# One piece of W per step, contexts loaded ahead of the layouts, and two parts of W's rounding moved from VectorE to GpSimd

## The chip, the cores and the metric

The kernel runs on one core of a Trainium2 chip (trn2). The metric is the device time of one execution in microseconds (us). Three executions of the kernel before took 529.82, 531.11 and 535.19 us, median 531.11 us; a fourth, profiled one took 529.71 us.

## The reference

For each of 16 items b (256 rows, 256 columns):

```
x1  = x + attention(layernorm(x), ctx, ctx)         # 16 heads of 16 columns, softmax over 256 keys
out = x1 + ffn(layernorm(x1))
ffn(z) = q(silu(q(z) @ q(w_gate).T) * (q(z) @ q(w_up).T)) @ q(w_down).T
q(z):  per block of 16 columns   scale = max(max|z| / 6, 1e-12)
       z/scale rounded to the grid 0, .5, 1, 1.5, 2, 3, 4, 6 with its sign, times scale
```

The weights w_gate and w_up (704 x 256) and w_down (256 x 704) have to go through q once. The change is about this quantisation of the weights.

## The kernel before

**Stages.** Attention runs first (about the first 285 us of the trace), the feed-forward part over 32 tiles of 128 rows after it. Attention is a software pipeline of steps t = -3 to 16. In step t, TensorE (PE) computes, head by head, the scores of item t (L1098) and, 22 heads ahead, the raw scores of items t+1 and t+2 from which VectorE (DVE) takes row maxima (L1112 and L783, `max_scores` and `maximum`). ScalarE (ACT) takes exponents (L611), PE multiplies by the values (L1130, one call of 16 matmuls per four heads). Every engine walks the same grid of positions (g, j), g and j from 0 to 3, one head per position; a few other operations are hung on given positions. There are two PSUM banks MX: `max_scores` of a head waits until the maximum of the head two before it is taken.

**The order on each engine is the program's.** A wait holds up everything behind it on that engine. The only DMA queue is that of SyncE (SP).

**SP, step t:** wait for GpSimd's third part of the keys of item t+3 (`k_low`), issue 6 DMAs of 128 KB that stack them (L300, KS<-KP); wait for the transposed maxima, issue one small DMA (L368, QS<-MT), without which PE can't start step t+1; wait for the third part of the queries of item t+3 (`q_out`, which ACT makes at position (3, 3), its last), issue 6 DMAs (L300, QS<-QP); then the layouts of item t+5 (L285 QN and L287 KT), the context of item t+2 (L290 C), the rows of item t (L293 X), and what is due of the weights. As `q_out` comes at the end of step t, everything from the query stack on is issued while PE, DVE, ACT and GpSimd (POOL) are already in step t+1.

**Loads of W, before:** w_gate before and in step -1; w_up 384 KB at the end of SP's step 0 and 256 + 64 KB at the end of step 1; w_down 352 KB each at the end of steps 2 and 3.

**W's quantisation.** W has 4608 columns (gate, up, down, each 1536), cut into 16 slices of 288 columns. Slice t+1 is scaled in step t (offset SCALE = 1) and slice t is rounded in step t (offset GRID = 0):

- DVE at (1, 1): `weight_maxima` (L846, wmax); at (2, 2) `weight_limits` (L830 and L831); at (2, 3) `weight_inverses` (L835) and `round_weights` (L857, WC = max(WC, constant)); in steps -1 and 0 the three parts of the scaling stand at (3, 3).
- ACT at (0, 3): WC = |W| * constant (L652).
- POOL near the end of its step: W + WC (L486), - WC (L489), * scale (L492); then W * inverse of the next slice (L498).

POOL's step t in order: add the attention result to x (L443 twice), KR (L450), small statistics (L456 to L461), the third key part KP (L465, which gives `k_low`), the values VA from the context (L471), then the four of W.

**Step 15** has no further maxima. In it PE transposes W into 14 lots (L1144, one at each of the first 14 positions), ACT and DVE copy them out (L680, L862). Lots 11 to 13 need slice 15 finished (`w_done`). Two early steps of the feed-forward part's preparation stand before step 15 on every engine.

Of the kernel before, what the change touches and what calls it, by code (L numbers as in the profile page):

```python
# [92 lines left out]
def program(nc, x, x_p, ctx_in, ctx_t, wg_in, wu_in, wd_in, out):  # L93
# [8 lines left out]
    with es:  # L102
# [6 lines left out]
        def sem(name):  # L109
            return es.enter_context(nc.semaphore(name))  # L110
# [74 lines left out]
        def bank(p):  # L185
# [28 lines left out]
        o_den, o_norm, x1_ready = sem("o_den"), sem("o_norm"), sem("x1_ready")  # L214
        w_zeroed, w_begun, w_loaded = sem("w_zeroed"), sem("w_begun"), [sem(f"w_loaded{m}") for m in range(3)]
        w_seq, w_scaled, w_abs, w_c, w_grid, w_done = (sem(n) for n in
            ("w_seq", "w_scaled", "w_abs", "w_c", "w_grid", "w_done"))
        ones_ready, ones_last = sem("ones_ready"), sem("ones_last")
        w_tr, w_out = sem("w_tr"), sem("w_out")
# [63 lines left out]
        def _(sp):  # L283
# [22 lines left out]

            def load_last(m, w):
                full = FI // 128
                sp.dma_start(WN[m][0:FI - full * 128, full, :], w[full * 128:FI, :]).then_inc(w_loaded[m], 16)

            def load_down(r):
                sp.dma_start(WD[:, r, 0:FI], wd_in[128 * r:128 * (r + 1), :]).then_inc(w_loaded[2], 16)

            def load_weights(t):

                if t == -1:
                    load_blocks(0, wg_in, 2, 5, w_loaded[0])
                    load_last(0, wg_in)
                if t == 0:
                    load_blocks(1, wu_in, 0, 3, w_loaded[1])  # L320
                if t == 1:
                    load_blocks(1, wu_in, 3, 5, w_loaded[1])
                    load_last(1, wu_in)
                if t in (2, 3):
                    load_down(t - 2)

# [29 lines left out]
            def attention_step(st):  # L356
                if st.has(LEAD):
                    r = st.slot(LEAD, RING)
                    sp.wait_ge(k_low, st.times(LEAD, 1, 1))
                    gate(sp)  # L360
                    sp.wait_ge(sc_ready, st.times(0, H, 1))
                    gate(sp)
                    stack(KS[r], KP[st.slot(LEAD, 2)], (0, 1, 2, 0, 1, 0), r)
                if st.has(1):
                    sp.wait_ge(mt_ready, st.times(1, 1, 1))
                    gate(sp)
                    r = st.slot(1, 2)
                    sp.dma_start(QS[st.slot(1, RING)][PROD:ROWS, :, :].rearrange("d h t -> d (h t)"),  # L368
                                 MT[r][:, :]).then_inc(m_stacked[r], 16)
                if st.first == -1:  # L370
                    load_context(1, 1)
                    load_weights(-1)
                if st.has(LEAD):
                    sp.wait_ge(q_out, st.times(LEAD, 3, 3))
                    gate(sp)
                    stack(QS[r_q(st)], QP[st.slot(LEAD, 2)], (0, 0, 0, 1, 1, 2), r_q(st))
                if st.has(LOADS):
                    load_first(st.item(LOADS), st.slot(LOADS, RING))
                if st.first >= 0 and st.has(2):
                    load_context(st.item(2), st.slot(2, RING))  # L380
                if st.has(0):
                    load_x(st.item(0), st.slot(0, RING))
                if st.first >= 0:
                    load_weights(st.first)

# [10 lines left out]

            steps(sp, attention_step, -1, RING, 1, RING, B - 1, B)
            attention_step(Step(B - 1, B, RING))
            attention_step(Step(B, B, RING))
            ffn_steps(sp, ffn_step)  # L400
# [4 lines left out]
        def _(pool):  # L405
# [30 lines left out]
            def attention_step(st):  # L436
# [40 lines left out]
                if st.first == -1:  # L477
                    pool.wait_ge(v_ready, 1)
                    pool.wait_ge(m_parts, 1)
                    rows_of_ones((2,))  # L480
                if st.has(GRID):

                    ws = wslice(st, GRID)
                    pool.wait_ge(w_c, st.times(GRID, 1, 1))
                    gate(pool)
# [8 lines left out]
                if st.has(SCALE):  # L494
                    ws = wslice(st, SCALE)
                    pool.wait_ge(w_seq, st.times(SCALE, 4, 4))
                    gate(pool)
# [274 lines left out]
        def _(dve):  # L772
# [53 lines left out]

            def limits(amax, scale, inv, sem_, per, first, st, off):

                dve.wait_ge(sem_, st.times(off, per, first))
                nc.vector.tensor_scalar(scale, amax, 1 / 6, TINY, ALU.mult, ALU.max).then_inc(sem_, 1)  # L830
                nc.vector.tensor_scalar(inv, amax, UP / 6, TINY * UP, ALU.mult, ALU.max).then_inc(sem_, 1)  # L831

            def invert(inv, sem_, per, first, st, off):
                dve.wait_ge(sem_, st.times(off, per, first + 2))
                nc.vector.reciprocal(inv, inv).then_inc(sem_, 1)  # L835

            def weight_maxima(st):
# [3 lines left out]
                elif st.first == 0:  # L841
                    dve.wait_ge(w_loaded[0], 32)
# [6 lines left out]
            def weight_limits(st):  # L849
                limits(wmax[:, :], wscale[st.slot(SCALE, 2)][:, :], winv[:, :], w_seq, 4, 1, st, SCALE)  # L850
# [27 lines left out]
            def attention_step(st):  # L878
# [3 lines left out]
                for g in range(NG):  # L882
                    for j in range(HG):
                        maximum(st, g, j)
                        if (g, j) == (0, 3) and st.has(LEAD) and st.first > 2 - LEAD:
                            statistics(st)
                            aggregate(st)
                        if (g, j) == ((1, 1) if st.first > 0 else (3, 3)) and st.has(SCALE):
                            weight_maxima(st)
# [6 lines left out]
                        if (g, j) == ((2, 2) if st.first > 0 else (3, 3)) and st.has(SCALE):  # L896
                            weight_limits(st)
# [7 lines left out]
                        if (g, j) == (3, 3) and st.first == RING:  # L905
                            dve.wait_ge(w_loaded[2], 32)
                        if st.first == B - 1 and HG * g + j < LOTS:
# [426 lines left out]
```

## Time and profile before

| | |
|---|---|
| median of 3 executions | 531.11 us (529.82 to 535.19) |
| profiled execution, its own time | 529.71 us |
| its span, first to last instruction | 527.9 us |
| mean granted TensorE clock | 0.981 |
| busy: PE, DVE, ACT, POOL | 92%, 82%, 71%, 57% of the span |
| PE matmuls | 4036, 486.9 us |
| DVE row maxima L783 | 256, 164.2 us |
| DMA moved | 48.97 MB, all of it but instructions on one queue |

Each share is a mean over the whole span. Attention and the feed-forward part each have their own limit, and in attention the first steps, the middle ones and the last have theirs; so the numbers that matter are those of single steps. A row of a timeline gives start and duration in us, the engine, the line of the kernel, the operation and its tiles, how many instructions are merged (x6) and, in brackets, how long the engine sat idle before it and what ended that. SPq is SP's queue of DMA issues: its rows are the times that SP spends on issuing, not those of the transfers.

### The profile page before, as it was taken

Reading aid. Unit: us, or ns where it says so; the run is one execution under the profiler, and the core shown is the slowest. Engines: PE = TensorE matmul, PEld = TensorE weight load, DVE = VectorE, ACT = ScalarE, POOL = GpSimd, SP = SyncE. Lnnn points to the kernel's source line nnn. Section 1 sums busy time; section 2 is a strip of 40 time slices with the busy share of each in tenths; the row PEclk is TensorE's granted clock in tenths of the full one; section 3 lists DMA queues with packets and bytes.
Section 4 is the critical chain, followed back from the end, with each engine's and each line's share of the span. In section 5 each row is a group of like instructions: output and inputs, shape, how many; then the busy total and the mean of one; then the engine's idle time right before and its main releaser. Section 6 shows DMA issues by size and latency. Waiting matters only on the chain.

```text
span 527.9 us, 13628 instructions
## 1 busy us (share of the span) xinstructions
PE 486.9 (92%) x4036; PEld 383.1 (73%) x4036; DVE 435.1 (82%) x1129; ACT 373.8 (71%) x740; POOL 302.3 (57%) x423
## 2 busy tenths in 40 slices
PE   1889899999999999997857899999999999999996
PEld 0245565666666666654437899999999999999996
DVE  3788899899999999886345888898889998889764
ACT  5569899999999999977653565556656566665653
POOL 7754465556566665443144566666676666766542
PEclk9999999999999999999877899999999999999999
DMA  7784878766666666521000000000000000000000
GB/s 215 215 220 126 212 197 220 226 192 178 191 185 182 176 186 179 149 88 43 0 2 0 2 21 20 10 20 20 20 20 10 20 20 20 20 10 21 23 21 30
DMA packets 49985, 48.97 MB, mean 93 GB/s; under 512 B 4768, under 2 KB 47648, under 8 KB 49952
## 3 DMA queue, kind: packets, MB, share of 16 engines
q1 hardware_dynamic: 49952, 48.58, 32.8%
q8 instruction: 15, 0.25, 0.2%
q14 instruction: 18, 0.15, 0.1%
HBM read 18.94 MB, written 4.19 MB: 44 GB/s over the span
## 4 chain that ended last, share of the span: by engine, by line
PE 73%; DVE 7%; issue 5%; POOL 4%; SPq 4%; ACT 4%; DMA 3%; POOLq 0%; DVEq 0%; ACTq 0%
PE SC L1182 22%; PE PV L1182 12%; PE PV L1130 9%; PE MX L1112 9%; PE SC L1098 7%; DVE MF L783 4%; PE T L1207 4%; SPq L300 3%; DMA QS<-MT 2%; PE T L1212 2%; PE T L1077 2%; PE T L1045 2%; PE SC L1207 1%; PE T L1052 1%; ACT P L611 1%
## 5 line engine op out<-in xcount | busy, mean ns | idle before, releaser
L783 DVE TENSOR_REDUCE MF<-MX 128x2 f32<-128x512 f32 x256 | 164.2, 685 | 19.0 <-PE MX L1112 16.2
L611 ACT ACTIVATE P<-SC 128x512 f32<-128x512 f32 x256 | 140.3, 594 | 19.8 <-PE SC L1098 17.8
L1112 PE MATMUL MX<-KS,QS 96*128 96x256 bf16 x512 | 102.9, 284 | 4.3 <-DVE MF L783 2.5
L1098 PE MATMUL SC<-QS,KS 98*128 98x256 bf16 x512 | 98.5, 274 | 3.6 <-DMA QS<-MT 3.5
L534 POOL TENSOR_TENSOR HQ<-HN,hscale 128x704 f32<-128x704 f32 x31 | 43.1, 1391 | 61.3 <-DVE HN L936 61.3
L716 ACT ACTIVATE HH<-T 128x768 fp32r<-128x768 f32 x31 | 25.2, 813 | 67.9 <-PE T L1207 67.9
L1130 PE MATMUL PV<-P,VA 128*32 128x256 f32 x1024 | 70.0, 392 | 0.9 <-ACT OT L620 0.9
L1098 PEld LDWEIGHTS SC<-QS,KS 98*128 98x128 bf16 x512 | 43.4, 97 | 35.7 <-ACT P L611 20.0
L1182 PE MATMUL SC<-WH,XH 128*128 128x352 f32 x256 | 68.7, 350 | 0.0
L1112 PEld LDWEIGHTS MX<-KS,QS 96*128 96x128 bf16 x512 | 43.9, 99 | 31.6 <-DVE MF L783 23.3
L1182 PE MATMUL SC<-WH,XL 128*128 128x352 f32 x256 | 62.9, 327 | 0.0
L1182 PE MATMUL SC<-WL,XH 128*128 128x352 f32 x256 | 62.9, 327 | 0.0
L1130 PEld LDWEIGHTS PV<-P,VA 128*32 128x32 f32 x1024 | 27.3, 110 | 25.6 <-ACT P L611 7.1
L1182 PEld LDWEIGHTS SC<-WL,XH 128*128 128x128 f32 x256 | 45.6, 192 | 0.0
L1182 PEld LDWEIGHTS SC<-WH,XL 128*128 128x128 f32 x256 | 45.3, 191 | 0.1
L521 POOL TENSOR_TENSOR HN<-HN,hinv 128x704 f32<-128x704 f32 x31 | 43.1, 1390 | 1.0 <-DVE hinv L1026 0.9
L916 DVE TENSOR_TENSOR HN<-SC,SG 128x352 f32<-128x352 f32 x64 | 33.3, 521 | 11.3 <-PE SC L1182 10.1
L1182 PEld LDWEIGHTS SC<-WH,XH 128*128 128x128 f32 x256 | 41.4, 194 | 1.6
L685 ACT ACTIVATE SG<-SC 128x352 f32<-128x352 f32 x64 | 29.4, 460 | 18.0 <-PE SC L1182 13.4
L529 POOL TENSOR_TENSOR frstd<-fve,mhalf 128x2 f32<-128x2 f32 x32 | 22.1, 691 | 22.5 <-DVE fve L983 22.5
L486 POOL TENSOR_TENSOR W<-W,WC 128x288 f32<-128x288 f32 (+1 forms) x16 | 12.7, 796 | 38.8 <-DVE WC L857 38.8
L576 ACT ACTIVATE QP<-T 128x512 bf16<-128x512 f32 x48 | 28.6, 595 | 6.5 <-PE T L1052 3.6
(138 smaller groups left out, 1029.8 us busy)
## 6 DMA issues: line engine op xcount, KB each, us to landing
KS<-KP SPq DMA_DIRECT2D x96, 128.0 KB, 3.1
QS<-QP SPq DMA_DIRECT2D x96, 128.0 KB, 2.4
QN<-in_x_p SPq DMA_DIRECT2D x16, 256.0 KB, 3.1
KT<-in_ctx_t SPq DMA_DIRECT2D x16, 256.0 KB, 3.1
C<-in_ctx SPq DMA_DIRECT2D x16, 256.0 KB, 4.2
X<-in_x SPq DMA_DIRECT2D x16, 256.0 KB, 4.9
out<-OB SPq DMA_DIRECT2D x32, 128.0 KB, 1.7
W<-in_L_ffn_w_down SPq DMA_DIRECT2D x2, 352.0 KB, 6.0
```

The lines of the kernel that those rows point to most:

```text
L521: nc.gpsimd.tensor_tensor(blocks(HN[r][:, :]), blocks(HN[r][:, :]), each(hinv[r][:, :]), ALU.mult).then_inc(hm_ready, 1)
L534: nc.gpsimd.tensor_tensor(blocks(HQ[r][:, 0:FI]), blocks(HN[r][:, :]), each(hscale[r][:, :]), ALU.mult).then_inc(hq_ready, 1)
L576: nc.scalar.activation(parts[:, n, :], bank, ACT.Copy).then_inc(out_sem, 1)
L611: nc.scalar.activation(P[g % 2][:, j, :, :], SC[h % 3][:, :, :], ACT.Exp, scale=0.25).then_inc(exp_done, 1)
L685: nc.scalar.activation(SG[a][:, :], G, ACT.Silu).then_inc(silu_done, 1)
L783: nc.vector.tensor_reduce(MF[st.slot(off, 2)][:, :, h:h + 1], MX[h % 2][:, :, :], AX.X, ALU.max, negate=True).then_inc(mx_done, 1)
L916: nc.vector.tensor_tensor(HN[st.slot(0, 2)][:, a * FH:(a + 1) * FH], U, SG[a][:, :], ALU.mult).then_inc(h_done, 1)
L1098: last = nc.tensor.matmul(SC[h % 3][:, k, :], KS[r][0:ROWS, h, k * 128:(k + 1) * 128], QS[r][0:ROWS, h, :], start=True, stop=True)
L1112: last = nc.tensor.matmul(MX[h % 2][:, q, :], QS[r][0:PROD, h, q * 128:(q + 1) * 128], KS[r][0:PROD, h, :], start=True, stop=True)
L1130: last = nc.tensor.matmul(PV[32 * j:32 * (j + 1), g % 2, :], VA[r][:, k, HG * g + j, :], P[g % 2][:, j, k, :], start=(k == 0), stop=(k == ...
L1182: mm = nc.tensor.matmul(dst, x[:, c, :], w[:, c, :], start=(first and i == 0), stop=(last and i == len(chunks) - 1))
L1207: return nc.tensor.matmul(dst, src, ident[:, :], start=first, stop=False, is_transpose=True, skip_group_check=True)
```

## The change

Weights are loaded in pieces of one block (128 KB; w_down in halves of a row block), one at the end of each of SP's steps 1 to 8, 10 and 11. At the end of SP's step t-1, SP waits until the piece issued one step earlier has landed and raises `w_ready` to t. In step t (from 1 on) DVE waits at (1, 1) for `w_ready` >= t before it takes the maxima of slice t+1; before, it waited in steps 0, 4 and for w_down in step 4 only. The context of item t+3 instead of t+2 is loaded, and before the layouts. Step 0's scaling moves from (3, 3) to (1, 1). DVE's `weight_limits` (two operations on 128x18) and `round_weights` (one on 128x288) go to POOL: the limits after VA and before the rounding of W, the rounding's max in front of L486; `weight_inverses` waits for them and stands at (3, 0). SP's steps are written out one by one without a loop.

```diff
+            PIECES = {t + 1: t for t in range(FI // 128 + 1)}
+            DOWN = {7: (0, 0, 384), 8: (0, 384, FI), 10: (1, 0, 384), 11: (1, 384, FI)}
+            def load_piece(t):
+                done = w_piece[t % 3]
+                if t in DOWN:
+                    load_down(*DOWN[t], done)
+                elif t in PIECES and PIECES[t] < FI // 128:
+                    load_blocks(1, wu_in, PIECES[t], PIECES[t] + 1, done)
+                elif t in PIECES:
+                    load_last(1, wu_in, done)
+            def piece_landed(t):
+                turns = sum(1 for u in (*PIECES, *DOWN) if u <= t - 2 and u % 3 == (t - 2) % 3)
+                if turns:
+                    sp.wait_ge(w_piece[(t - 2) % 3], 16 * turns)
+                sp.sem_inc(w_ready, 1)
...
                     stack(QS[r_q(st)], QP[st.slot(LEAD, 2)], (0, 0, 0, 1, 1, 2), r_q(st))
+                if st.has(LEAD):
+                    load_context(st.item(LEAD), st.slot(LEAD, RING))
                 if st.has(LOADS):
                     load_first(st.item(LOADS), st.slot(LOADS, RING))
-                if st.first >= 0 and st.has(2):
-                    load_context(st.item(2), st.slot(2, RING))
                 if st.has(0):
                     load_x(st.item(0), st.slot(0, RING))
-                if st.first >= 0:
-                    load_weights(st.first)
+                load_piece(st.first)
+                if 1 <= st.first + 1 < B:
+                    piece_landed(st.first + 1)
...
-            steps(sp, attention_step, -1, RING, 1, RING, B - 1, B)
-            attention_step(Step(B - 1, B, RING))
-            attention_step(Step(B, B, RING))
+            for t in range(-1, B + 1):
+                attention_step(Step(t, B, RING))
...
+                if st.has(SCALE):
+                    pool.wait_ge(w_seq, st.times(SCALE, 2, 1))
+                    pool.wait_ge(w_scaled, st.times(SCALE, 1))
+                    gate(pool)
+                    nc.gpsimd.tensor_scalar(wscale[st.slot(SCALE, 2)][:, :], wmax[:, :], 1 / 6, TINY,
+                                            ALU.mult, ALU.max).then_inc(w_lim, 1)
+                    nc.gpsimd.tensor_scalar(winv[:, :], wmax[:, :], UP / 6, TINY * UP, ALU.mult, ALU.max).then_inc(w_lim, 1)
                 if st.has(GRID):
                     ws = wslice(st, GRID)
+                    pool.wait_ge(w_abs, st.times(GRID, 1, 1))
+                    gate(pool)
+                    nc.gpsimd.tensor_scalar(WC[:, :], WC[:, :], MAGIC * ONE, None, ALU.max).then_inc(w_c, 1)
...
-                elif st.first == RING:
-                    dve.wait_ge(w_loaded[1], 48)
+                else:
+                    dve.wait_ge(w_ready, st.times(0, 1))
...
             def weight_inverses(st):
-                invert(winv[:, :], w_seq, 4, 1, st, SCALE)
-            def round_weights(st):
-                dve.wait_ge(w_abs, st.times(GRID, 1, 1))
-                nc.vector.tensor_scalar(WC[:, :], WC[:, :], MAGIC * ONE, None, ALU.max).then_inc(w_c, 1)
+                dve.wait_ge(w_lim, st.times(SCALE, 2, 2))
+                nc.vector.reciprocal(winv[:, :], winv[:, :]).then_inc(w_seq, 1)
...
-                        if (g, j) == ((1, 1) if st.first > 0 else (3, 3)) and st.has(SCALE):
+                        if (g, j) == ((1, 1) if st.first >= 0 else (3, 3)) and st.has(SCALE):
                             weight_maxima(st)
...
-                        if (g, j) == ((2, 3) if st.first > 0 else (3, 3)) and st.has(SCALE):
+                        if (g, j) == ((3, 0) if st.first >= 0 else (3, 3)) and st.has(SCALE):
                             weight_inverses(st)
-                        if (g, j) == (2, 3) and st.has(GRID):
-                            round_weights(st)
```

## Rows read from the trace of the kernel before

**Rows 1.** Timeline of PE: first score matmuls of steps 1 to 5, 8, 11, 12
```profile
47.34 0.39 PE L1098 MATMUL SC<-QS,KS 98*128 98x256 bf16 x2 [0.66 <-DMA QS<-MT]
...
63.14 0.39 PE L1098 MATMUL SC<-QS,KS 98*128 98x256 bf16 x2 [1.50 <-DMA QS<-MT]
...
77.46 0.39 PE L1098 MATMUL SC<-QS,KS 98*128 98x256 bf16 x2 [0.22 <-DMA QS<-MT]
...
92.52 0.39 PE L1098 MATMUL SC<-QS,KS 98*128 98x256 bf16 x2 [0.94 <-DMA QS<-MT]
...
106.95 0.39 PE L1098 MATMUL SC<-QS,KS 98*128 98x256 bf16 x2 [0.19 <-DMA QS<-MT]
...
149.03 0.39 PE L1098 MATMUL SC<-QS,KS 98*128 98x256 bf16 x2
...
191.16 0.39 PE L1098 MATMUL SC<-QS,KS 98*128 98x256 bf16 x2
...
205.17 0.39 PE L1098 MATMUL SC<-QS,KS 98*128 98x256 bf16 x2
```

**Rows 2.** Timeline of SP's DMA issues while PE is in step 8
```profile
149.25 3.80 SPq L300 DMA_DIRECT2D QS<-QP  x6
153.10 0.60 SPq L285 DMA_DIRECT2D QN<-in_x_p  x1
...
154.76 0.47 SPq L293 DMA_DIRECT2D X<-in_x  x1
156.38 3.81 SPq L300 DMA_DIRECT2D KS<-KP  x6
160.40 0.67 SPq L368 DMA_DIRECT2D QS<-MT  x1
```

**Rows 3.** Timeline of SP's DMA issues while PE is in step 1
```profile
50.84 1.44 SPq L285 DMA_DIRECT2D QN<-in_x_p  x1
...
54.16 0.46 SPq L304 DMA_DIRECT2D W<-in_L_ffn_w_up  x1
...
58.79 0.68 SPq L368 DMA_DIRECT2D QS<-MT  x1
```

**Rows 4.** Timeline of DVE around position (1, 1) of step 8
```profile
153.22 1.29 DVE L783 TENSOR_REDUCE MF<-MX 128x2 f32<-128x512 f32 x2
154.43 0.44 DVE L846 TENSOR_REDUCE wmax<-W 128x18 f32 x1
154.99 2.61 DVE L783 TENSOR_REDUCE MF<-MX 128x2 f32<-128x512 f32 x4
```

**Rows 5.** Timeline of PE at positions (2, 0) and (2, 1) of step 8
```profile
155.89 0.38 PE L1112 MATMUL MX<-KS,QS 96*128 96x256 bf16 x2
156.11 0.38 PE L1098 MATMUL SC<-QS,KS 98*128 98x256 bf16 x2
156.33 0.39 PE L1112 MATMUL MX<-KS,QS 96*128 96x256 bf16 x2
```

**Rows 6.** Groups by line: the moved rounding step, POOL's nearest operations
```profile
L857 DVE TENSOR_SCALAR WC<-WC 128x288 f32<-128x288 f32 x16 | 4.2, 261 | 0.0
L471 POOL TENSOR_SCALAR VA<-C 128x512 f32<-128x512 f32 x16 | 10.0, 622 | 36.9 <-DMA C<-in_ctx 30.4 <-PE PV L1130 5.2 <-issue 1.4
L456 POOL TENSOR_SCALAR ve<-mv 128x2 f32<-128x2 f32 x15 | 3.5, 231 | 7.4 <-DVE mv L798 7.2
```

**Rows 7.** Timeline of POOL at the start of step 0 (before PE's step 1)
```profile
33.98 0.68 POOL L498 TENSOR_TENSOR W<-W,winv 128x288 f32<-128x288 f32 x1 [2.73 <-DVE winv L835]
```

**Rows 8.** Timelines at the end of step 14 and in step 15: POOL, DVE, PE, ACT
```profile
246.68 0.71 POOL L529 TENSOR_TENSOR frstd<-fve,mhalf 128x2 f32<-128x2 f32 x1
...
245.70 0.15 DVE L983 TENSOR_SCALAR fve<-fmv 128x1 f32<-128x1 f32 x1
...
250.22 0.87 PE L1144 MATMUL MX<-ident,W 128*128 128x128 f32 x3 [2.46 <-DVE WL L862]
...
265.17 0.44 PE L1144 MATMUL MX<-ident,W 128*128 128x128 f32 x2 [2.71 <-POOL W L492]
...
252.05 0.43 ACT L652 ACTIVATE WC<-W 128x288 f32<-128x288 f32 x1
```

**Rows 9.** Busy time by stretch: stretch, length, PE (count), PEld, DVE, ACT, POOL, PE clock, DMA share, GB/s
```profile
250.10:253.50 3.40, 3.28 (x24) 1.99 (x24) 1.05 (x2) 1.89 (x5) 1.96 (x4) 0.50 0.00 0
```

More of the change, by code:

```diff
@@ L214, in program @@
         o_den, o_norm, x1_ready = sem("o_den"), sem("o_norm"), sem("x1_ready")
-        w_zeroed, w_begun, w_loaded = sem("w_zeroed"), sem("w_begun"), [sem(f"w_loaded{m}") for m in range(3)]
+        w_zeroed, w_begun, w_loaded, w_ready = sem("w_zeroed"), sem("w_begun"), sem("w_loaded"), sem("w_ready")
+        w_piece = [sem(f"w_piece{r}") for r in range(3)]
         w_seq, w_scaled, w_abs, w_c, w_grid, w_done = (sem(n) for n in
             ("w_seq", "w_scaled", "w_abs", "w_c", "w_grid", "w_done"))
-        ones_ready, ones_last = sem("ones_ready"), sem("ones_last")
+        ones_ready, ones_last, w_lim = sem("ones_ready"), sem("ones_last"), sem("w_lim")
         w_tr, w_out = sem("w_tr"), sem("w_out")
@@ L305, in load_blocks, with load_last, load_down @@
                              ).then_inc(done, 16)
-            def load_last(m, w):
+            def load_last(m, w, done):
                 full = FI // 128
[L309 to L325, printed above, removed]
+                sp.dma_start(WN[m][0:FI - full * 128, full, :], w[full * 128:FI, :]).then_inc(done, 16)
+            def load_down(r, lo, hi, done):
+                sp.dma_start(WD[:, r, lo:hi], wd_in[128 * r:128 * (r + 1), lo:hi]).then_inc(done, 16)
+            PIECES = {t + 1: t for t in range(FI // 128 + 1)}
[13 more added lines that the diff above has]
+                sp.sem_inc(w_ready, 1)
             def part(dst, parts, p, rows, r):
@@ L371, in attention_step @@
                     load_context(1, 1)
-                    load_weights(-1)
+                    load_blocks(0, wg_in, 2, 5, w_loaded)
+                    load_last(0, wg_in, w_loaded)
                 if st.has(LEAD):
@@ L495, in attention_step @@
                     ws = wslice(st, SCALE)
-                    pool.wait_ge(w_seq, st.times(SCALE, 4, 4))
+                    pool.wait_ge(w_seq, st.times(SCALE, 2, 2))
                     gate(pool)
@@ L825, in output @@
                                         ALU.mult).then_inc(o_norm, 1)
[L827 to L835, printed above, removed]
             def weight_maxima(st):
@@ L841, in weight_maxima @@
                 elif st.first == 0:
-                    dve.wait_ge(w_loaded[0], 32)
-                elif st.first == RING:
-                    dve.wait_ge(w_loaded[1], 48)
+                    dve.wait_ge(w_loaded, 32)
+                else:
+                    dve.wait_ge(w_ready, st.times(0, 1))
                 dve.wait_ge(w_scaled, st.times(SCALE, 1))
@@ L847, in weight_maxima @@
                                         apply_absolute_value=True).then_inc(w_seq, 1)
-            def weight_limits(st):
-                limits(wmax[:, :], wscale[st.slot(SCALE, 2)][:, :], winv[:, :], w_seq, 4, 1, st, SCALE)
             def weight_inverses(st):
-                invert(winv[:, :], w_seq, 4, 1, st, SCALE)
-            def round_weights(st):
-                dve.wait_ge(w_abs, st.times(GRID, 1, 1))
-                nc.vector.tensor_scalar(WC[:, :], WC[:, :], MAGIC * ONE, None, ALU.max).then_inc(w_c, 1)
+                dve.wait_ge(w_lim, st.times(SCALE, 2, 2))
+                nc.vector.reciprocal(winv[:, :], winv[:, :]).then_inc(w_seq, 1)
             def weights_out(n):
@@ L895, in attention_step @@
                             maxima_low(st)
-                        if (g, j) == ((2, 2) if st.first > 0 else (3, 3)) and st.has(SCALE):
-                            weight_limits(st)
                         if (g, j) == (3, 1) and st.has(-1):
@@ L900, in attention_step @@
                             output(st, 1)
-                        if (g, j) == ((2, 3) if st.first > 0 else (3, 3)) and st.has(SCALE):
+                        if (g, j) == ((3, 0) if st.first >= 0 else (3, 3)) and st.has(SCALE):
                             weight_inverses(st)
-                        if (g, j) == (2, 3) and st.has(GRID):
-                            round_weights(st)
-                        if (g, j) == (3, 3) and st.first == RING:
-                            dve.wait_ge(w_loaded[2], 32)
                         if st.first == B - 1 and HG * g + j < LOTS:
```

## The prediction

> **What bounds the kernel now.** I read the timeline of PE first, step by step, because the mean shares hide three different stretches. In the middle of attention a step takes 14.01 us (from 191.16 to 205.17) and PE shows no idle time at its start [rows 1]: PE is the bound. The early steps are longer: step 1 takes 15.80 us (47.34 to 63.14), step 2 14.32, step 3 15.06, step 4 14.43, and each next step begins after PE idled for the small DMA of the maxima (1.50, 0.22, 0.94, 0.19 us) [rows 1]. The timeline of SP shows why in step 1: this DMA is issued at 58.79 and 4.35 us pass until the scores of step 2 start at 63.14 [rows 1], behind a 384 KB load of w_up issued at 54.16 [rows 3]; in step 8, without a load of weights, it is issued at 160.40, 11.4 us after the step's start at 149.03 [rows 1, 2], and the next step isn't late. The last stretch is step 15, where PE stands still twice for W's path: 2.46 us for a copy by DVE and 2.71 us for GpSimd's last operation on slice 15 [rows 8].
>
> **Part 1, loads in pieces.** The early steps lose their late landings: step 1 can fall from 15.80 to 14.1 (-1.7), step 2 by 0.2, step 3 by 1.0 and step 4 by 0.4, in sum -3.3 us, of which the bounds are 0 (all of it comes from issues that ran long, as the 1.44 us one at 50.84 [rows 3], which nothing here takes away) and -3.3. I take the whole, because the part in PE's brackets (1.50 + 0.22 + 0.94 + 0.19 = 2.85 us) is nearly as much. In the middle steps a piece adds one issue of 0.46 us [rows 3] to SP. SP has room for it as regards the key stack: it is idle from 155.23 (154.76 + 0.47) to 156.38 [rows 2].
>
> **Part 2, the new wait.** This is the largest term. DVE waits at (1, 1) of step t for `w_ready` = t, which SP gives at the end of its step t-1. SP's step t-1 does not end before the others' step t begins: its query stack waits for ACT's last query part. In step 8 the stack is issued from 149.25 (0.22 us after PE's start of the step), takes 3.80 us, and layouts, context and rows follow until 155.23 [rows 2]. The change reorders these four and adds the piece: 0.05 + 0.46 us more. So the release comes at about 155.8 with a piece and 155.3 without. DVE is at (1, 1) at 154.43, where wmax starts [rows 4]. It is held for 1.4 or 0.9 us.
>
> What is behind the wait on DVE: the maximum of (1, 2), now at 154.99. wmax takes 0.44 and the maximum can follow 0.05 later, so it starts at 156.3 (with a piece) or 155.8: 1.3 or 0.8 us later, as 0.1 us of slack lies between 154.87 and 154.99 [rows 4]. Who waits for that: `max_scores` needs the bank of the head two before. Four maxima take 2.61 us, one every 0.64; that of (1, 3) ends near 156.3, and PE's matmuls at (2, 1) start at 156.33 [rows 4, 5]. There is no slack at all. So PE is late by the full 1.3 or 0.8 us, and as it is the bound, and all that follows on it is in order, the step gets longer by that. DVE, which is late no more after it has caught up, gives nothing back. The other bounds of this term: 0, if the release came in time, and 1.4 (the whole hold).
>
> How many: a piece is issued at the end of SP's steps 1 to 8, 10 and 11, that is during steps 2 to 9, 11 and 12. Steps 2 to 9 and 11: 9 x 1.3 = 11.7. Step 10, no piece: 0.8. In step 12 there are no layouts left to load (1.1 us less before the release): 0.3. In step 1 PE starts 0.66 us late against the query stack [rows 1] and there is no piece: 0.3. Steps 13 and 14: none, two loads or fewer. Sum +13.1 us.
>
> The DMA page of the Trainium skill ("DMA: Bandwidth & Descriptors", section on the anatomy of one DMA, told there of GpSimd's path) gives about 50 ns for the sequencer's dispatch of a DMA. If that were what an issue costs SP here, the ten or eleven issues would take an estimated 0.6 us, the release would come long before DVE, and the sum would lose this whole term. The trace disagrees: six issues take 3.80 us and SP's next one starts after them [rows 2].
>
> **Part 3, contexts earlier.** GpSimd's VA waited 30.4 us in all for the context [rows 6]. What waits for VA and the work behind it on GpSimd was late nowhere but at W's rounding. Zero in the middle steps; it lets GpSimd reach the new limits in time. If a context still came late, the key part KP is ahead of VA and would hide it.
>
> **Part 4, DVE to GpSimd.** DVE saves 0.26 us a step for WC [rows 6] and the two small limits. PE was the bound, so I put 0 on that; with the wait it is idle time. On GpSimd the max on 128x288 costs between 0.23 (2 columns) and 0.62 us (512 columns) [rows 6]; by columns 0.45. It is hidden: the limits can start when wmax ends, near 156.4, and DVE asks for them only at (3, 0), three maxima after (2, 1), past 160. In step -1 there is no cover: DVE's maxima, GpSimd's two limits and DVE's inverse follow each other at (3, 3), and GpSimd had waited 2.73 us for the inverse anyway [rows 7]. Two limits at 0.23 in place of DVE's own small operations, and two hand-overs: +0.4 us (bounds 0 and 0.9), which DVE's chain to the statistics and to `k_low` passes on to step 1.
>
> The Trainium skill ("GPSIMD Engine Reference", section on elementwise work) says that GpSimd is the wrong engine for plain elementwise work, roughly half as fast as DVE. By it the max takes an estimated 0.5 us, and it speaks against this part. The trace agrees on the direction, but off the path the sum stays.
>
> **Part 5, the end.** In step 15 GpSimd no longer waits for DVE at (2, 3). |W| is ready at 252.05 + 0.43 [rows 8], one max, three operations and gaps of 0.2 later, near 256, slice 15 is done: the stall of 2.71 us goes. In step 14 GpSimd is free before DVE's fve; frstd starts 0.7 us earlier (246.68 against 245.70 + 0.15 and a hand-over) [rows 8], and the first stall shrinks by as much. Sum -3.4. PE ran at half of full speed (1.2 instead of 2.4 GHz) from 250.1 to 253.5, after the first stall, with 3.28 us of matmuls [rows 9]. A stall shorter or at another moment may save 1.6 us of it or bring another such stretch; I take 0 and keep +-1.6.
>
> **Sum.** -3.3 + 13.1 + 0.4 - 3.4 = +6.8 us. Against the profiled execution's own 529.71 us that is 536.5. The median shown is 1.4 us above it, so I predict 538 us, 1.3% slower.
>
> **Rivals.** (a) The release is in time, for instance because SP's issue rows overlap what follows, as by the page cited above. Then -3.3 + 0.4 - 3.4 = -6.3: 525 us. For it: GpSimd's and SP's other waits are all planned with room. Against it: the order of SP's rows. The break-even is a mean hold of 6.3/11 = 0.57 us per step. (b) The hold is there but half of it is absorbed, because PE's start at (2, 1) has slack that merged rows hide: +6.5 instead of +13.1, 531 us. (c) More than forecast: issues that ran long (1.44 instead of 0.60 us at 50.84 [rows 3]) now lengthen the hold one for one, and early gains stay out: +2 to +5, 541 us. A late limit at (3, 0) would fall in this case too; nothing speaks for it.
>
> **How the numbers follow.** Forecast (536 to 540) 0.54, (a) 0.22, (b) 0.12, (c) 0.12. One per cent, about what can be told from no change, is 5.3 us: 525.8 to 536.4. Faster: 0.21, nearly all of (a). Same: (b), a piece of (a) and the lower edge of the forecast, 0.19. Slower: 0.60. The range goes from 526, which leaves out most of (a), to 543. As both signs have weight: the forecast's own range is 535 to 541.
>
> **What would show it.** Right: DVE idle 0.8 to 1.4 us before wmax in steps 2 to 11, with nothing or SP named as releaser; steps of 14.8 to 15.3 us; no idle time before wmax in steps 13 and 14; VA no longer waiting for C; no stall of PE at the eleventh lot. Part 1: the maxima's DMA in steps 1 to 4 lands as in step 8. Wrong: steps 2 to 9 of 14.0 us and DVE not idle before wmax, which is case (a), or DVE held and the step still 14.0, which is (b).

## The result and the profile after

Four executions of the changed kernel took 538.32, 543.45, 543.49 and 544.52 us, median 543.5 us; the kernel before, beside it, 531.85 us. The ratio is 1.019, with a 95% interval from 1.011 to 1.028: slower, as forecast, clear of noise; whether by more than 2% can't be told. By the medians it is 11.6 us where 6.8 were forecast, and half a microsecond above the upper end of the range; by the ratio it is 10.3 us. Medians here and below are over all executions, while ratios and their intervals leave out those in a slow state, so that the two can differ by some tenths of a per cent. The profiled execution is the one of 544.52 us, so the comparison of the two traces has 14.8 us to explain.

The wait that Part 2 put its largest term on is there. These are the rows of the waits of the changed kernel (who waited, for whom: us in total, times, longest):

```profile
PEld MX L1109 <- DVE MF L802: 41.0, 76, 2.6
DVE wmax L855 <- SPq L333: 18.5, 13, 2.8
PE MX L1109 <- DVE MF L802: 15.5, 20, 2.3
```

DVE's wait for SP's release, called a hold from here on, is 18.5 us in 13 waits (steps 1 to 13), and PE's waits for a row maximum follow from it: 15.5 us by its matmuls, 41.0 by its weight loads, most of which overlap matmuls. The chain of the work that ended last, followed back from the last instruction, says the same by shares of the span:

```profile
PE 62%; SPq 13%; ACT 8%; issue 8%; DVE 6%; POOL 2%; DMA 1%; DVEq 0%; ACTq 0%; POOLq 0%
```

SP's queue has 13% of it, after 4% in the kernel before. The stacks (SP's L301) alone have 8% of it.

Step by step it can be read in PE's timeline. The first scores of steps 1, 2, 3, 5, 6 and 12, to be set beside [rows 1]:

```profile
49.02 0.39 PE L1095 MATMUL SC<-QS,KS 98*128 98x256 bf16 x2
68.30 0.39 PE L1095 MATMUL SC<-QS,KS 98*128 98x256 bf16 x2
86.56 0.39 PE L1095 MATMUL SC<-QS,KS 98*128 98x256 bf16 x2
...
117.21 0.39 PE L1095 MATMUL SC<-QS,KS 98*128 98x256 bf16 x2
132.63 0.39 PE L1095 MATMUL SC<-QS,KS 98*128 98x256 bf16 x2
...
224.34 0.39 PE L1095 MATMUL SC<-QS,KS 98*128 98x256 bf16 x2
```

Step 1 takes 19.28 us, step 2 18.26, step 5 15.42. None of these rows has idle time in brackets any more: PE is no longer late at the start of a step, but in the middle of it. The account, profile to profile (after minus before; stretches from the first scores of a step, the last two cut at W's first transpose):

| stretch | before, us | after, us | change | forecast |
|---|---|---|---|---|
| up to step 1 | 47.3 | 49.0 | +1.7 | +0.4 |
| steps 1 and 2 | 30.1 | 37.5 | **+7.4** | -0.3 |
| steps 3 and 4 | 29.5 | 30.7 | +1.2 | +1.2 |
| steps 5 to 11 | 98.2 | 107.1 | +8.9 | +8.6 |
| steps 12 to 14 | 41.1 | 41.8 | +0.7 | +0.3 |
| the rest | 281.6 | 276.6 | -5.0 | -3.4 |

From step 3 to step 14 the forecast holds within 0.4 us a stretch. It missed most in steps 1 and 2, by 7.7 us, and by 1.3 before step 1; the rest gained 1.6 more than forecast.

**A middle step.** SP during PE's step 5, which starts at 117.21 (these rows are the end of SP's own step 4):

```profile
117.44 3.79 SPq L301 DMA_DIRECT2D QS<-QP  x6
121.27 0.60 SPq L291 DMA_DIRECT2D C<-in_ctx  x1
121.92 0.50 SPq L286 DMA_DIRECT2D QN<-in_x_p  x1
122.46 0.47 SPq L288 DMA_DIRECT2D KT<-in_ctx_t  x1
122.97 0.44 SPq L294 DMA_DIRECT2D X<-in_x  x1
123.45 0.47 SPq L305 DMA_DIRECT2D W<-in_L_ffn_w_up  x1
```

The issues of SP's step 4 end at 123.92, 6.7 us after PE began step 5. DVE in the same step:

```profile
121.41 1.29 DVE L802 TENSOR_REDUCE MF<-MX 128x2 f32<-128x512 f32 x2
124.22 0.45 DVE L855 TENSOR_REDUCE wmax<-W 128x18 f32 x1 [1.52 <-SPq L333]
```

and PE at (2, 1), its next matmuls for the maxima:

```profile
125.33 0.39 PE L1109 MATMUL MX<-KS,QS 96*128 96x256 bf16 x2 [1.10 <-DVE MF L802]
```

DVE starts wmax 0.3 us after the last issue ended. It had idled 1.52 us; PE stands still for 1.10 of them at this row, and the step has grown by 1.4 us, from 14.01 to 15.42 (where PE loses the last 0.3 the rows do not single out).

**Steps 1 and 2.** SP there:

```profile
49.33 5.00 SPq L301 DMA_DIRECT2D QS<-QP  x6
54.37 0.59 SPq L291 DMA_DIRECT2D C<-in_ctx  x1
55.41 0.37 SPq L286 DMA_DIRECT2D QN<-in_x_p  x1
...
68.46 5.21 SPq L301 DMA_DIRECT2D QS<-QP  x6
```

The six issues take 5.00 and 5.21 us instead of 3.79, and in step 1 there are 0.45 us between the context's row (it ends at 54.96) and QN's. All of it lies before the release, and DVE is held longer by as much:

```profile
57.07 0.45 DVE L855 TENSOR_REDUCE wmax<-W 128x18 f32 x1 [2.55 <-SPq L333]
...
76.54 0.45 DVE L855 TENSOR_REDUCE wmax<-W 128x18 f32 x1 [2.76 <-SPq L333]
```

And what follows costs more than the hold. PE's row behind the first of them, then two stretches with the busy time of PE, PEld, DVE, ACT and POOL (with the number of instructions), the granted clock, the DMA share and GB/s:

```profile
58.18 0.61 PE L1109 MATMUL MX<-KS,QS 96*128 96x256 bf16 x2 [2.13 <-DVE MF L802]
```

```profile
57.60:64.40 6.80, 6.22 (x35) 3.37 (x35) 4.49 (x10) 2.17 (x4) 3.79 (x6) 0.51 0.78 191
78.00:81.40 3.40, 3.40 (x25) 2.04 (x26) 3.16 (x8) 1.57 (x3) 2.73 (x4) 0.54 1.08 283
```

For 10.2 us PE runs at the lower of its two levels, 1.2 instead of 2.4 GHz, after it had stood still for 2.13 us in step 1 and for 2.33 us (its row at 77.65) behind the hold of 2.76 us in step 2. Its matmuls fill nearly all of that time, so what they lose is lost for the step.

**Before step 1.** The clock has a part here too. The first 16 matmuls by the values in step 0, in the kernel before and in the changed one:

```profile
36.52 1.07 PE L1130 MATMUL PV<-P,VA 128*32 128x256 f32 x16
```

```profile
38.26 1.94 PE L1127 MATMUL PV<-P,VA 128*32 128x256 f32 x16
```

The changed kernel's take 1.94 us instead of 1.07, and its pairs for the scores 0.63 to 0.64 instead of 0.38 to 0.39 until about 40.5: PE is at the lower level in the first 8 us of step 0, where the kernel before is at the upper one.

**The tail.** PE's rows of W's transposes in step 15, to be read beside [rows 8]:

```profile
269.32 0.79 PE L1141 MATMUL MX<-ident,W 128*128 128x128 f32 x3 [1.73 <-DVE WL L865]
...
283.16 0.41 PE L1141 MATMUL MX<-ident,W 128*128 128x128 f32 x2 [0.19 <-DVE WDL L865]
```

The first stall is 1.73 us instead of 2.46, shorter by the 0.7 us that was forecast, and the one of 2.71 us is gone.

**GpSimd.** Its groups over the whole kernel (count, busy us, mean ns, idle before and what ended it):

```profile
L480 POOL TENSOR_SCALAR VA<-C 128x512 f32<-128x512 f32 x16 | 9.9, 620 | 7.7 <-issue 6.7 <-DMA C<-in_ctx 1.1
L502 POOL TENSOR_SCALAR WC<-WC 128x288 f32<-128x288 f32 x16 | 15.0, 937 | 1.7 <-ACT WC L671 0.5
L494 POOL TENSOR_SCALAR wscale<-wmax 128x18 f32<-128x18 f32 x16 | 4.8, 301 | 9.0 <-DVE wmax L855 8.1
```

VA waits 1.1 us for its context instead of 30.4 [rows 6]. The max on 128x288 takes 937 ns, outside the bounds of Part 4, but no other engine waited for it.

### The profile page after: what moved, and what is told of

Same layout as the page of the kernel before. It is cut to its first block, busy times and chain, and to the rows that moved or that the text cites. A ratio compares the mean times of both kernels' runs of the same rounds, so it can differ in the third digit from the quotient of the medians.

```text
span 542.7 us, 13665 instructions
## 1 busy us (share of the span) xinstructions
PE 495.1 (91%) x4036; PEld 385.3 (71%) x4036; DVE 431.4 (79%) x1081; ACT 375.4 (69%) x740; POOL 327.7 (60%) x471
## 4 chain that ended last, share of the span: by engine, by line
PE 62%; SPq 13%; ACT 8%; issue 8%; DVE 6%; POOL 2%; DMA 1%; DVEq 0%; ACTq 0%; POOLq 0%
PE SC L1179 21%; PE PV L1179 12%; SPq L301 8%; PE MX L1109 6%; PE PV L1127 6%; PE SC L1095 4%; ACT P L630 4%; PE T L1204 4%; DVE MF L802 4%; PE T L1209 2%; PE T L1042 2%; ACT QP L595 2%; SPq L291 1%; PE SC L1204 1%; SPq L286 1%
## 5 line engine op out<-in xcount | busy, mean ns | idle before, releaser
L1109 PE MATMUL MX<-KS,QS 96*128 96x256 bf16 x512 | 106.1, 292 | 17.5 <-DVE MF L802 15.5
L1095 PE MATMUL SC<-QS,KS 98*128 98x256 bf16 x512 | 101.2, 280 | 0.0
L1109 PEld LDWEIGHTS MX<-KS,QS 96*128 96x128 bf16 x512 | 45.1, 101 | 48.3 <-DVE MF L802 41.0
L1127 PE MATMUL PV<-P,VA 128*32 128x256 f32 x1024 | 72.5, 403 | 0.9 <-ACT OT L639 0.9
L1095 PEld LDWEIGHTS SC<-QS,KS 98*128 98x128 bf16 x512 | 44.6, 99 | 33.4 <-ACT P L630 18.1
L913 DVE TENSOR_TENSOR HN<-SC,SG 128x352 f32<-128x352 f32 x64 | 33.3, 520 | 10.3 <-PE SC L1179 9.2
L459 POOL TENSOR_TENSOR KR<-KT,KP 128x512 f32<-128x512 f32 x15 | 17.4, 1160 | 32.8 <-ACT KP L604 32.6
```

Of the source, the lines that this page charges most:

```text
L913: nc.vector.tensor_tensor(HN[st.slot(0, 2)][:, a * FH:(a + 1) * FH], U, SG[a][:, :], ALU.mult).then_inc(h_done, 1)
L1095: last = nc.tensor.matmul(SC[h % 3][:, k, :], KS[r][0:ROWS, h, k * 128:(k + 1) * 128], QS[r][0:ROWS, h, :], start=True, stop=True)
L1109: last = nc.tensor.matmul(MX[h % 2][:, q, :], QS[r][0:PROD, h, q * 128:(q + 1) * 128], KS[r][0:PROD, h, :], start=True, stop=True)
L1127: last = nc.tensor.matmul(PV[32 * j:32 * (j + 1), g % 2, :], VA[r][:, k, HG * g + j, :], P[g % 2][:, j, k, :], start=(k == 0), stop=(k == ...
```

## The experiments

Two theories stood against each other. **A**: the wait for SP's late release makes the middle steps longer, and where SP is later still, in steps 1 and 2, TensorE's slower stretches come on top. **B**: the cost lies elsewhere, in SP's longer list of issues, in GpSimd's new work, or in loads that are now spread thin. The ratios are to the kernel before beside each run (its medians are 531.0 us in the first batch, 530.5 in the second).

### The release without the late place

```diff
+                if 1 <= st.first + 1 < B:
+                    piece_landed(st.first + 1)
                 if st.has(LEAD):
                     sp.wait_ge(q_out, st.times(LEAD, 3, 3))
...
                 load_piece(st.first)
-                if 1 <= st.first + 1 < B:
-                    piece_landed(st.first + 1)
```

SP still waits for the earlier piece and raises `w_ready`, but before it waits for the queries, that is in its own step.

> The changed kernel with SP's wait for the piece and the raising of w_ready moved ahead of SP's wait for the last query part; all else as changed. Theory (the hold at (1,1) costs 1.33 us in each of the middle steps): the release then comes some 12 us into the step before, DVE is never held, the middle steps go back from 15.35 to 14.03 us, and the kernel takes about 525 us against 531 (ratio 0.985 to 0.993). Rival 1 (GpSimd's added operations, or DVE's wait for GpSimd's limits, lengthen the steps): steps stay near 15.3, 540 to 543 us. Rival 2 (the pieces' transfers lengthen the steps): as rival 1, 540 us.

Measured: 524.6 us, ratio 0.989 (0.9855 to 0.9924). No hold is left, most middle steps take 14.01 to 14.08 us, steps 1 and 2 together 30.9 (there with 3.4 us at the lower clock, from 65.9 on, though nothing held DVE). SP in the step of this kernel that starts near 108:

```profile
108.22 3.80 SPq L301 DMA_DIRECT2D QS<-QP  x6
...
114.24 0.47 SPq L305 DMA_DIRECT2D W<-in_L_ffn_w_up  x1
```

and DVE:

```profile
113.98 0.44 DVE L855 TENSOR_REDUCE wmax<-W 128x18 f32 x1
```

DVE takes the maxima before the piece of this step has even been issued: every piece had landed in time, and nothing but the place of the release held DVE. SP gets to this place when its issue of the transposed maxima ends, at 106.85, which is 1.7 us before PE's step starts at 108.58; in the changed kernel it got there 6.7 us after the start. This version beats both kernels. The second one puts the release one wait later, directly behind the query stack.

```diff
                     stack(QS[r_q(st)], QP[st.slot(LEAD, 2)], (0, 0, 0, 1, 1, 2), r_q(st))
+                    if 1 <= st.first + 1 < B:
+                        piece_landed(st.first + 1)
...
-                if 1 <= st.first + 1 < B:
-                    piece_landed(st.first + 1)
```

> The changed kernel with the release directly behind the six DMAs of the query stack, ahead of context, layouts, rows and piece. Theory: the release comes about 0.25 + 3.8 us into the step, DVE is at (1,1) at 5.4, so no hold, the same as with the early release within 1 us (about 525 us); only where six issues take 5.0 us or more is DVE held a few tenths. Rivals 1 and 2: 540 us as the changed kernel.

Measured: 525.6 us, 0.991 (0.9872 to 0.9954), again without a hold; steps 1 and 2 take 28.6 us together. The two are not told apart: no room beyond the second place, 4.0 us into the step, is needed.

### The wait alone, in the kernel before

```diff
                 if st.first >= 0:
                     load_weights(st.first)
+                if 1 <= st.first + 1 < B:
+                    sp.sem_inc(w_ready, 1)
...
+                if st.first > 0:
+                    dve.wait_ge(w_ready, st.times(0, 1))
```

SP raises the semaphore without waiting for anything; loads, contexts and GpSimd's work are those of before.

> The kernel before, with one thing added: SP raises w_ready at the end of each of its steps, and DVE waits for it at (1,1) as in the changed kernel; loads, order and GpSimd's work as before. Theory: DVE held 0.9 us in steps 5 to 11 and 1.4 to 2 us in steps 1 to 4, where a load of weights stands ahead of the release; 0.8 us for each of steps 5 to 11 and 3 us in steps 1 to 4, in sum +8 to +10 us: 539 to 541 us. Rivals 1 and 2: no change, 531 us.

Measured: 541.8 us, 1.020 (1.012 to 1.029), as much as the whole changed kernel costs, with none of its other parts. The waits, then SP and DVE in a middle step:

```profile
DVE wmax L850 <- SPq L386: 13.0, 10, 3.1
```

```profile
118.79 3.78 SPq L300 DMA_DIRECT2D QS<-QP  x6
...
124.28 0.47 SPq L293 DMA_DIRECT2D X<-in_x  x1
...
125.04 0.45 DVE L850 TENSOR_REDUCE wmax<-W 128x18 f32 x1 [1.00 <-SPq L386]
```

Without a piece the hold is 1.00 us here (0.84 to 1.02 in the middle steps) and a middle step takes 14.8 to 14.9: the 0.8 us of growth that Part 2 gave to steps without a piece. Steps 1 and 2, where this kernel issues w_up's large loads, have holds of 2.73 and 3.12 us, lengths of 19.44 and 18.46 us, and 10.2 us at the lower clock, the picture seen in the changed kernel. B is refuted as the main cause.

### The piece ahead of the release or behind it

```diff
-                load_piece(st.first)
                 if 1 <= st.first + 1 < B:
                     piece_landed(st.first + 1)
+                load_piece(st.first)
```

> The changed kernel with the release one DMA issue earlier, between the rows X and the piece of W. Theory (each issue ahead of the release is paid one for one by PE): DVE is held 0.9 to 1.0 instead of 1.45 us in steps 3 to 9 and 11, these steps take 14.85 instead of 15.35 us, in sum -4.5 us: 539 us. Rival (some of the hold is absorbed, or the length comes from elsewhere): less than 1 us of change, 543 us.

Measured: 535.3 us, 1.010 (1.0063 to 1.014). SP and DVE in a middle step:

```profile
148.37 0.55 SPq L310 DMA_DIRECT2D W<-in_L_ffn_w_up  x1
...
148.47 0.45 DVE L855 TENSOR_REDUCE wmax<-W 128x18 f32 x1 [0.91 <-SPq L333]
```

One issue of 0.5 us taken out from before the release shortens the hold from 1.5 to 0.9 us and most middle steps by 0.5, to 14.75 to 14.94. The hold is priced by what SP issues, one for one. The total fell by 8.2 us by the medians and by 4.8 by the ratios, where 4.5 were expected; the two intervals are too wide to say more. In the profile steps 1 and 2 came to 33.7 instead of 37.5 us as well, with holds of 2.12 and 2.35 us and 3.4 us at the lower clock instead of 10.2.

### Steps 1 and 2

Only the DVE waits of steps 1 and 2 are left out (the slices taken there, 2 and 3, lie in w_gate, which is loaded long before; DVE's steps -3 to 4 are written out one by one for it):

```diff
-                else:
+                elif st.first > 2:
                     dve.wait_ge(w_ready, st.times(0, 1))
```

> The changed kernel, but DVE waits for w_ready only from step 3 on (DVE's steps 1 to 4 are written out for that; nothing in steps 1 and 2 needs a piece). Theory A (in steps 1 and 2 the hold of 2.55 and 2.76 us, with the half-speed stretches of TensorE that follow, makes up what the forecast missed): steps 1 and 2 together fall from 37.5 to about 31 us, no half-speed stretch between 57 and 82 us, and the kernel takes 536 to 538 us against 543.5. Theory B (SP's DMA issues that run long, or the loads, lengthen steps 1 and 2 with or without the wait): 541 to 544 us.

Measured: 535.7 us, 1.0075 (1.004 to 1.011). PE's first scores of steps 1, 2 and 3:

```profile
50.07 0.39 PE L1095 MATMUL SC<-QS,KS 98*128 98x256 bf16 x2
64.10 0.39 PE L1095 MATMUL SC<-QS,KS 98*128 98x256 bf16 x2
78.64 0.39 PE L1095 MATMUL SC<-QS,KS 98*128 98x256 bf16 x2 [0.46 <-DMA QS<-MT]
```

28.6 us for both steps instead of 37.5, and no stretch at the lower clock from step 1 on in attention. Between these two profiles, two holds of the thirteen cost 9.0 us. They hold DVE for 5.3 us together; the other 3.7 us are what is left for the stretches at the lower clock, by subtraction. Against the second profile of the changed kernel, below, the same two holds cost 4.4 us, so the 9.0 are no fixed price.

Then both kernels once more, unchanged, with a profile, to see how much of this is the same every time.

> The changed kernel, unchanged, for a second profile. DVE held 2.5 to 2.8 us in steps 1 and 2, and 1.4 to 1.5 in steps 3 to 9 and 11, as in the first. If the half-speed stretches of TensorE in steps 1 and 2 follow from the long holds they come again between 57 and 82 us; if they were chance, steps 1 and 2 together take about 34 instead of 37.5 us.

Measured: 538.9 us. Steps 1 and 2 took 17.62 and 15.32 us, steps 3 to 9 15.3 to 15.4. DVE, PE and a window of this execution:

```profile
56.93 0.45 DVE L855 TENSOR_REDUCE wmax<-W 128x18 f32 x1 [2.11 <-SPq L333]
...
73.86 0.45 DVE L855 TENSOR_REDUCE wmax<-W 128x18 f32 x1 [1.42 <-SPq L333]
```

```profile
58.04 0.39 PE L1109 MATMUL MX<-KS,QS 96*128 96x256 bf16 x2 [1.69 <-DVE MF L802]
```

```profile
59.20:62.60 3.40, 3.40 (x26) 1.62 (x25) 2.62 (x6) 1.57 (x3) 2.35 (x4) 0.55 0.98 216
```

No issue ran long in step 2, so its hold is that of a middle step, and the lower clock lasts 3.4 us instead of 10.2 in steps 1 and 2. The same program takes 538.3 to 538.9 or 543.5 to 544.5 us. Of these, two were profiled, and steps 1 and 2 account for 4.6 of the 5.7 us between them. In the changed kernel SP's own irregularity shows up as time. The clock fell in step 0 of this execution as well: after a stall of PE of 1.44 us (0.88 at the same place before) it is at the lower level from 35.3 to 42.1.

> The kernel before, unchanged, for a second profile. In the first one TensorE's matmuls ran at full speed from 31.5 us on (16 matmuls of PV in 1.07 us at 36.5) and step 1 began at 47.3; in all nine other profiles so far those 16 took 1.3 to 1.9 us and step 1 began at 48.3 to 50.1. Theory A (the first profile happened to reach full speed early, whatever the kernel): here the first PV group takes 1.9 us and step 1 begins at 48.5 to 50. Theory B (the change's step -1 and 0 cost 1 us or more): 1.07 us and 47.3 again.

Measured: 530.6 us. The question was whether the first profile had reached full speed early by chance. It had not: the first 16 matmuls by the values take 1.07 us again and step 1 begins at 47.84, 1.2 us before that of the first profile of the changed kernel and 1.5 before that of the second.

```profile
37.05 1.07 PE L1130 MATMUL PV<-P,VA 128*32 128x256 f32 x16
...
47.84 0.39 PE L1098 MATMUL SC<-QS,KS 98*128 98x256 bf16 x2 [0.63 <-DMA QS<-MT]
```

In this execution, too, a query stack runs long, the one of step 2 with 4.87 us:

```profile
62.09 4.87 SPq L300 DMA_DIRECT2D QS<-QP  x6
...
77.99 3.79 SPq L300 DMA_DIRECT2D QS<-QP  x6
```

Issues that run long are thus no product of the change; before, DVE did not wait for them, and the granted clock was 1.00 from 57 to 64 us and from 78 to 85.

### The other parts alone

GpSimd's part alone, in the kernel before:

```diff
-                            weight_limits(st)
...
-                            round_weights(st)
...
+                    nc.gpsimd.tensor_scalar(wscale[st.slot(SCALE, 2)][:, :], wmax[:, :], 1 / 6, TINY,
+                                            ALU.mult, ALU.max).then_inc(w_lim, 1)
+                    nc.gpsimd.tensor_scalar(winv[:, :], wmax[:, :], UP / 6, TINY * UP, ALU.mult, ALU.max).then_inc(w_lim, 1)
...
+                    nc.gpsimd.tensor_scalar(WC[:, :], WC[:, :], MAGIC * ONE, None, ALU.max).then_inc(w_c, 1)
```

> The kernel before with the limits and the rounding's max made by GpSimd and the inverses at (3,0), and nothing else of the change. Theory: no stall of PE at lot 11 (2.71 us) and 0.7 us less at lot 2, 0.4 us more in step 0: -3 us, 528 us, ratio 0.994. Rival 1: +8 to +10 us. Rival 2: -3 us as the theory.

Measured: 527.8 us, 0.996 (0.9917 to 1.0001), so the gain itself is hardly clear of noise; the stalls in the trace are. PE's first stall in step 15 is 1.73 us and the one at the eleventh lot is gone, as in the changed kernel: Part 5 and the middle of Part 4 stand.

The same with the contexts one step earlier and ahead of the layouts:

```diff
+                if st.has(LEAD):
+                    load_context(st.item(LEAD), st.slot(LEAD, RING))
                 if st.has(LOADS):
                     load_first(st.item(LOADS), st.slot(LOADS, RING))
-                if st.first >= 0 and st.has(2):
-                    load_context(st.item(2), st.slot(2, RING))
```

> The kernel before with GpSimd's part of the change (as in e4) and the contexts one step earlier and ahead of the layouts; weights loaded as before, no w_ready. Theory: VA no longer waits for the context, but nothing that bounds a step waited for it, so the same as GpSimd's part alone within 1 us: 528 us (ratio to before 0.994). Rival: part of the early gain of 3.2 us between e4 and e1 comes from the contexts: 525 to 526 us.

Measured: 528.3 us, 0.995 (0.991 to 0.9985). 31.4 us of VA's waits fall to 0.8 and no time goes with them: contexts are worth nothing that can be measured, as Part 3 had it. The kernel with the early release is this one plus the pieces. By the ratios it takes 3.0 us less, near Part 1's term (-3.3), but the two intervals together leave some 2.7 us to either side (an estimate from their widths).

### Another cure: the maxima later

```diff
-                        if (g, j) == ((1, 1) if st.first >= 0 else (3, 3)) and st.has(SCALE):
+                        if (g, j) == ((2, 2) if st.first > 0 else (1, 1) if st.first == 0 else (3, 3)) and st.has(SCALE):
```

The release stays late; DVE asks for it four positions later.

> The changed kernel with SP's late release kept, but DVE's maxima of W (and with them the wait) at (2,2) in place of (1,1) in steps 1 to 14. Theory: DVE is there some 9.6 us into the step, the release comes at 6.7, so no hold; GpSimd's two limits then end at about 11.5 us, where (3,0) asks for them, so up to 0.3 us a step may come back as a hold there: 525 to 529 us. Rival (GpSimd or the transfers are the cause): 540 us or more.

Measured: 530.6 us, 1.000 (0.9964 to 1.0035), outside what was expected. The holds are gone and steps 5 to 12 sum to 113.9 us, as with the release behind the stack (113.8). The larger part of the loss is at the end: from W's first transpose to the last instruction it takes 278.8 us, against 274.9 with the release behind the stack. GpSimd in step 14, with PE's stall after it:

```profile
245.81 0.30 POOL L494 TENSOR_SCALAR wscale<-wmax 128x18 f32<-128x18 f32 x1 [5.92 <-DVE wmax L855]
...
250.90 0.73 POOL L548 TENSOR_TENSOR frstd<-fve,mhalf 128x2 f32<-128x2 f32 x1
```

```profile
254.46 0.73 PE L1141 MATMUL MX<-ident,W 128*128 128x128 f32 x3 [4.11 <-DVE WL L865]
```

GpSimd now stands 5.92 us at the limits, finishes its W work late and gives frstd, the first operation of the feed-forward part's statistics, only at 250.9; DVE's copy waits for what hangs on it and PE stalls 4.11 us instead of 1.73. The wait had not gone, it had moved to the next engine (50.8 us of GpSimd waiting for wmax in all), where it is free in the middle and paid for at the end.

## Why the prediction was right in direction and too small in size

**Part 1** (-3.3): not visible in the changed kernel itself, whose steps 1 and 2 grew, and borne out in the main by the versions without a hold. The kernel with pieces and early release is 3.0 us faster, by the ratios, than the one without pieces. Steps 1 to 4 take 57.4 us in the profile with pieces and the release behind the stack, against 59.6 and 60.7 in the two of the kernel before. In the profile with the early release they take 60.2, with a stall of 1.08 us for the maxima's DMA and a stretch at the lower clock, so that not every early step was cured.

**Part 2** (+13.1): the mechanism is right in every link: the release 6.7 us after the step's start, holds of 1.42 to 1.53 us in steps 3 to 9 and 0.92 in step 10, steps longer by 1.4 and 0.9. The stretch from step 5 to 11 gave +8.9 for +8.6. Two small things were off: step 13, put at none, was held 0.29 us, and step 11, with a piece, 1.34 us. The term that was mis-sized is that of steps 1 and 2. Their growths were put at 0.3 and 1.3 us, -0.3 for both with Part 1's gain; measured were holds of 2.55 and 2.76 us and a growth of 7.4 us for both. Two things were missing. The first: step 1 was taken to have slack, because in the kernel before PE starts after the query stack. The 0.66 us in [rows 1] was read as that lead; it is PE's idle time, and the stack was issued at 47.00, 0.34 us before PE. In the changed kernel the stack starts 0.31 us after PE, and in the other steps looked at 0.16 to 0.23. The 1.44 us issue at 50.84 [rows 3] was read, and kept for the rival (c) at 12%, though it stood in the very stretch that the new wait made critical. The second: no term at all stood for TensorE's clock in attention (some 3.7 us in the profiled execution, by the subtraction above). [rows 9] had shown PE at 1.2 GHz after a stall of 2.46 us; holds of more than 2 us were not expected, and so this cost was not either.

**Rival (c)** is the case that came: long issues lengthen the hold one for one and the early gain stays out. Its size, +2 to +5 us, was short as well: the median lies 5.5 us above the forecast and the profiled execution 8.0; (c) had neither the clock in it nor the 1.3 us before step 1. The second profile of the changed kernel (538.9 us) comes close to the forecast of 538 partly by luck. Against the first profile of the kernel before it is 9.2 us longer, where the sum said 6.8: 1.6 us too much before step 1 and 3.1 in steps 1 and 2, of which the stretch after W's first transpose took back 3.0.

**Rival (a)** (525 us) needed a release in time. The Trainium skill ("DMA: Bandwidth & Descriptors", anatomy of one DMA, told there of GpSimd's path) gives some 50 ns for a dispatch. The piece that was moved behind the release took 0.55 us on SP and shortened the step by 0.5: no run agrees with 50 ns here, and 525 us is what the kernel takes only when the release itself is moved.

**Rival (b)** (half of the hold absorbed) did not come: in step 5 a hold of 1.52 us made the step 1.41 us longer.

**Part 3** (0): right, by the pair of kernels with and without it (528.3 and 527.8 us, ratios 0.995 and 0.996).

**Part 4**: 0 in the middle was right. The price of GpSimd's max was not: 937 ns against bounds of 230 and 620. The bounds were by columns, from two other operations; DVE took 261 ns for the same [rows 6]. Only where it was hidden was this harmless. The Trainium skill ("GPSIMD Engine Reference", engine selection) calls one-input operations on GpSimd roughly line-rate and two-input ones about twice as slow as DVE. The prediction's estimate of 0.5 us took the factor of two inputs for a max that has one; measured, this one-input max is 3.6 times as slow. The small term before step 1 was +0.4 and came out as +1.7. DVE does wait 0.89 us for GpSimd in step -1, and the clock adds to it: all ten profiles of other kernels than the one before have 3.4 us or more at the lower clock in step 0, the two profiles of the kernel before have next to none (under 0.5 us). GpSimd's new work can't be the whole reason, for the kernel with the wait alone has none of it, nor any wait before step 1, and still begins step 0 late (33.6) and is at the lower clock until about 42. Whether the change brings the clock down there or chance does stays open.

**Part 5** (-3.4): right, stall by stall (0.73 and 2.71 us). The rest of the kernel gained 1.6 us more, which is the bound that was kept for the clock:

```profile
269.20:272.60 3.40, 3.28 (x24) 1.92 (x24) 1.05 (x2) 1.89 (x5) 2.86 (x5) 0.53 0.02 5
289.70:299.90 10.20, 8.28 (x39) 6.28 (x40) 4.44 (x20) 4.14 (x8) 5.74 (x11) 0.51 0.01 2
```

These two stretches at 1.2 GHz are all that is left there, 13.6 us; before there were 20.5 us in three. That this is where the 1.6 us come from is likely, but no run shows it.

**Faster, same, slower**: 0.60 stood on slower, and by the ratio it is slower by 1.9%, with the whole interval above 1%. The upper end of the range, 543, was the forecast plus the 5 us that (c) allowed at most. It had no room for two long issues in a row with the clock behind them.

## What to carry to other kernels

A semaphore that is raised at the end of a queue's step is raised when that queue gets there, and a DMA queue whose last transfers wait for the last part of a step gets there in the middle of everybody else's next step: put the release where its condition is true (here 8 us earlier, with data that had landed by then), not where the list ends. When a wait is added to an engine that has no slack, look at every row that then stands before its release, and price the ones that ran long once already. And when a wait is moved later instead, ask who needs its result in the last step, where there is no next one to hide it.

## What the runs showed of the hardware

- Some DMA issues on SP take longer than their kind, in all kernels and at changing places, most of them in the first 115 us: stacks of six take 4.4 to 5.4 us there beside the usual 3.8, single issues now and then 0.8 to 2.1 us beside some 0.5. A few come later (a stack of 4.57 us at 222.05 with the early release). What makes them long was not tried and is open.
- After stalls of PE of 2.13, 2.33, 1.69 and 1.73 us in the changed kernel the granted clock was found at the lower level, for 3.4 or 6.8 us; after the 1.10 us of a middle step it stayed at the upper one. The length of a stall does not decide it: with GpSimd's part alone it stayed up after 1.69 us (at 55.85), with the release ahead of the piece after 1.70 (at 56.99), and in the second profile of the kernel before after the same 2.46 us stall that the lower clock followed in the first. In the kernel with the early release it fell 2.4 us after a stall of only 1.08 us (at 63.50). What decides it these runs do not show.
- GpSimd's speed differs by operation: 620 ns for 128x512 (VA), 937 ns for a max over 128x288, and 301 ns for 18 columns.
